# Local attention: the mask added by VectorE in the operation that takes the row extreme, instead of by mask products on TensorE

## What is computed

```python
q = l2norm(q) * qs
k = l2norm(k) * ksc
q, k = rotary_xpos(q, k)
...
bq = q.reshape(b, h, w, WINDOW, d) * QK_SCALE          # 8.0
bk, bv = (look_around(bk), look_around(bv))            # window before, window itself
sim = jnp.einsum('bhwid,bhwjd->bhwij', bq, bk)
mask = (i < j) | (i > j + WINDOW) | (j == -1)
sim = jnp.where(mask, -jnp.finfo(sim.dtype).max, sim)
attn = jax.nn.softmax(sim, axis=-1)
out = jnp.einsum('bhwij,bhwjd->bhwid', attn, bv)
```

## Time and profile before

| | |
|---|---|
| median of 3 runs | 2368.93 us (2366.84 to 2369.19) |
| profiled execution | 2361.52 us, its span 2359.7 us |
| busy: TensorE / VectorE / ScalarE / GpSimd | 1962.5 (83%) / 1318.0 (56%) / 1012.6 (43%) / 528.9 us (22%) |
| local attention, layer 0 and layer 1 | about 1103 to 1400 us and 1553 to 1850 us |
| L1369, two layers | 64 reductions, 1216 ns each |
| L1450, two layers | 256 exponentials, 483 ns each |
| L1568, score products, two layers | 512 TensorE instructions |

### The profile page before, as it was taken

The page is one execution under the profiler, slowest core; times in us unless marked ns, Lnnn a source line. Parts: engine busy times, 40 slices in busy tenths (PEclk is TensorE's granted clock), DMA queues, the critical chain, the costliest instruction groups (busy, mean ns, idle before and its releaser), DMA issues. The chain is left out here.

```text
span 2359.7 us, 32440 instructions
## 1 busy us (share of the span) xinstructions
PE 1962.5 (83%) x11804; PEld 1240.0 (53%) x11836; DVE 1318.0 (56%) x2301; ACT 1012.6 (43%) x2111; POOL 528.9 (22%) x893
## 2 busy tenths in 40 slices
PE   3788888888799797896899979979999899874595
PEld 1335555555467465574465655535566455442494
DVE  3548888888623498232666643236666333885412
ACT  1238888888621242211465641116565211432121
POOL 2102222222332300232222210112222110222321
PEclk9889999999999899998999999989999999986797
DMA  2243111110000100002000000030000000027395
GB/s 67 71 132 113 43 39 37 38 37 2 1 1 0 54 1 1 0 1 89 5 1 1 1 1 0 1 105 1 1 1 1 1 1 0 15 56 198 113 308 153
DMA packets 99133, 99.60 MB, mean 42 GB/s; under 512 B 33740, under 2 KB 83232, under 8 KB 98848
## 3 DMA queue, kind: packets, MB, share of 16 engines
q1 hardware_dynamic: 95904, 93.21, 13.2%
q0 software_dynamic: 3072, 4.34, 1.0%
HBM read 80.60 MB, written 16.92 MB: 41 GB/s over the span
## 5 line engine op out<-in xcount | busy, mean ns | idle before, releaser
L515 DVE TENSOR_REDUCE negmax<-sps 128x1 f32<-128x1024 f32 x256 | 307.6, 1212 | 21.6 <-PE sps L466 20.9
L559 ACT ACTIVATE prob<-sps,negmax 128x1024 f32<-128x1024 f32 x256 | 286.2, 1118 | 8.7 <-DVE negmax L515 6.1
L475 PE MATMUL sps<-ident,prob 128*128 128x128 f32 x1152 | 182.2, 287 | 57.0 <-ACT prob L559 56.1
L475 PEld LDWEIGHTS sps<-ident,prob 128*128 128x128 f32 x1152 | 134.7, 144 | 144.2 <-ACT prob L559 129.1
L604 POOL TENSOR_TENSOR probT<-probT,after 128x128 f32<-128x128 f32 x256 | 116.6, 455 | 281.5 <-DVE probT L523 191.3
L466 PE MATMUL sps<-ks,qs 128*128 128x512 f16 x512 | 162.1, 387 | 21.0 <-DVE ores L535 17.7
L568 ACT COPY probT<-sps 128x512 f32<-128x512 f32 (+1 forms) x192 | 101.6, 529 | 22.1 <-PE sps L475 22.1
L1304 POOL TENSOR_TENSOR la1qs<-la1qn,la1sin 128x256 f32<-128x256 f32 x64 | 60.3, 972 | 196.0 <-DVE la1qn L1381 196.0
L1304 POOL TENSOR_TENSOR la0qs<-la0qn,la0sin 128x256 f32<-128x256 f32 x64 | 60.3, 972 | 195.0 <-DVE la0qn L1381 195.0
L523 DVE COPY probT<-sps 128x512 f32<-128x512 f32 (+3 forms) x192 | 91.4, 476 | 4.7 <-PE sps L475 4.7
L491 PE MATMUL sps<-probT,vres 128*32 128x128 f32 x2304 | 82.5, 279 | 8.3 <-POOL probT L604 5.7
(11 more groups left out here) (450 smaller groups left out, 4246.2 us busy)
## 6 DMA issues: line engine op xcount, KB each, us to landing
w1e<-in_fc_T SPq DMA_DIRECT2D x16, 1024.0 KB, 6.6
w2e<-in_fc_T SPq DMA_DIRECT2D x16, 1024.0 KB, 9.6
qs<-q_parts SPq DMA_DIRECT2D x128, 64.0 KB, 1.9
ks<-k_parts SPq DMA_DIRECT2D x128, 64.0 KB, 1.9
q_parts<-parts SPq DMA_DIRECT2D x8, 512.0 KB, 3.6
k_parts<-parts SPq DMA_DIRECT2D x8, 512.0 KB, 5.4
token_rows<-r_row SPq DMA_DIRECT2D x4, 544.0 KB, 3.3
mixed<-r_zero SPq DMA_DIRECT2D x1, 2056.0 KB, 10.8
```

The lines of the kernel that those rows point to most:

```text
L475: mm = pe.transpose(slots[n % 4][:, at * P:(at + 1) * P], prob[:, n % 3, t * P:(t + 1) * P], ident[:])
L515: dve.tensor_reduce(negmax[:, n % 4:n % 4 + 1], slots[n % 4][:], X, ALU.max, negate=True).then_inc(s.max_done, 1)
L559: act.activation(prob[:, n % 3, :], slots[n % 4][:], ACT.Exp, bias=negmax[:, n % 4:n % 4 + 1], accum_out=rowsum[:, tile % 2, n % QUAD:n % ...
```

## The change

The scores' sign is turned: the table that holds the query scale has -8 in place of 8, so the scores come out negated, and masked places get +1e30 in place of -1e30. The mask products and the bf16 mask and identity tiles go. VectorE runs one fused operation per head: it adds the float32 mask to the head's 128 x 256 negated scores out of PSUM, writes the result to `prob` in SBUF, and gives the row's minimum to `nmax`. The minimum of the negated scores is the negated maximum, which the exponential takes as its bias as before; the exponential now reads and writes `prob` in place, with a scale of -1. `row_max` waits for the transposes that read `prob`, and `exponents` no longer does.

```diff
-        NEG = -1e30
+        FAR = 1e30
...
-                masks = sb(ph + "mb", [P, 2, 2, 2 * P], BF16, c)
-                identb = sb(ph + "ib", [P, P], BF16, c)
...
-                        pool.memset(maskf[:, 0, 0, :], NEG).then_inc(s.built2, 1)
+                        pool.memset(maskf[:, 0, 0, :], FAR).then_inc(s.built2, 1)
...
-                        pool.wait_ge(s.built2, 4)
-                        pool.tensor_copy(identb[:], ident[:]).then_inc(s.built3, 1)
-                        for first in range(2):
-                            for x in range(2):
-                                pool.tensor_copy(masks[:, first, x, :], maskf[:, first, :, :].rearrange("p a t -> p (a t)")).then_inc(s.built3, 1)
...
                                 dve.wait_ge(s.scores, 2 * t + half + 1)
-                                dve.tensor_reduce(nmax[:, half * HL // 2:(half + 1) * HL // 2],
-                                                  bs[:, half * 1024:(half + 1) * 1024].rearrange("p (s t) -> p s t", t=2 * P), X, ALU.max,
-                                                  negate=True).then_inc(s.max_done, 1)
+                                if t == 0 and half == 0:
+                                    dve.wait_ge(s.built2, 4)
+                                if t > 0:
+                                    dve.wait_ge(s.p_turned, 2 * t - 1 + half)
+                                for h in heads(half):
+                                    ins = dve.tensor_tensor_reduce(prob[:, h, :], bs[:, slot(h) * 256:(slot(h) + 1) * 256],
+                                                                   maskf[:, 1 if t % TPB else 0, :, :].rearrange("p a t -> p (a t)"),
+                                                                   1.0, FAR, ALU.add, ALU.min, nmax[:, h:h + 1])
+                                ins.then_inc(s.max_done, 1)
...
                             if t > 0:
                                 act.wait_ge(s.rinv_done, t)
-                                act.wait_ge(s.p_turned, 2 * t)
                             for half in range(2):
                                 act.wait_ge(s.max_done, 2 * t + half + 1)
                                 for h in heads(half):
-                                    ins = act.activation(prob[:, h, :], bs[:, slot(h) * 256:(slot(h) + 1) * 256], ACT.Exp,
-                                                         bias=nmax[:, slot(h):slot(h) + 1], accum_out=rsum[:, h:h + 1])
+                                    ins = act.activation(prob[:, h, :], prob[:, h, :], ACT.Exp, scale=-1.0,
+                                                         bias=nmax[:, h:h + 1], accum_out=rsum[:, h:h + 1])
...
-                            if t == 0:
-                                pe.wait_ge(s.built3, 5)
...
-                                for r in (2 * half, 2 * half + 1):
-                                    pe.matmul(bs[:, r * 512:(r + 1) * 512], identb[:],
-                                              masks[:, 1 if t % TPB else 0, :, :].rearrange("p x t -> p (x t)"),
-                                              start=True, stop=False, skip_group_check=True)
...
-                                                   start=False, stop=True, skip_group_check=True)
+                                                   start=True, stop=True, skip_group_check=True)
...
-    qk_scale = np.float32(8.0)
+    qk_scale = np.float32(-8.0)
```

More of the change, by code:

```diff
@@ L1232, in local_attention @@
                 bs = ps(ph + "bs", [P, 2048], c)
-                s = signals(ph, "@next_in @wo_in @w_in @tab_in @built1 @built2 @built3 @tab1 @x_turned @h_done @qk_done "
+                s = signals(ph, "@next_in @wo_in @w_in @tab_in @built1 @built2 @tab1 @x_turned @h_done @qk_done "
                             "@squared @ssum_done @norm_done @clipped @rnorm_done @normed @cos_done @sin_done "
@@ L1270, in _ @@
                         pool.wait_ge(s.built1, 5)
-                        pool.memset(maskf[:, 0, 0, :], NEG).then_inc(s.built2, 1)
-                        pool.affine_select(out=maskf[:, 1, 0, :], in_=maskf[:, 1, 0, :], compare_op=ALU.is_ge, fill=NEG,
+                        pool.memset(maskf[:, 0, 0, :], FAR).then_inc(s.built2, 1)
+                        pool.affine_select(out=maskf[:, 1, 0, :], in_=maskf[:, 1, 0, :], compare_op=ALU.is_ge, fill=FAR,
                                            base=0, pattern=[[1, P]], channel_multiplier=-1).then_inc(s.built2, 1)
                         for w in range(2):
-                            pool.affine_select(out=maskf[:, w, 1, :], in_=maskf[:, w, 1, :], compare_op=ALU.is_ge, fill=NEG,
+                            pool.affine_select(out=maskf[:, w, 1, :], in_=maskf[:, w, 1, :], compare_op=ALU.is_ge, fill=FAR,
                                                base=0, pattern=[[-1, P]], channel_multiplier=1).then_inc(s.built2, 1)
-                        pool.wait_ge(s.built2, 4)
-                        pool.tensor_copy(identb[:], ident[:]).then_inc(s.built3, 1)
-                        for first in range(2):
-                            for x in range(2):
-                                pool.tensor_copy(masks[:, first, x, :], maskf[:, first, :, :].rearrange("p a t -> p (a t)")).then_inc(s.built3, 1)
                         if l == 0:
```

## The result

| | before | after |
|---|---|---|
| median, runs on one chip | 2367.89 us (2365.28 to 2369.19) | 2398.64 us (2396.37 to 2400.94) |
| span of the profiled execution | 2359.7 us | 2396.8 us |
| mean granted clock of TensorE | 0.938 | 0.931 |
| busy: TensorE / VectorE / ScalarE / GpSimd | 1962.5 / 1318.0 / 1012.6 / 528.9 us | 1946.1 / 1333.5 / 1022.2 / 525.8 us |

The ratio is 1.0134, with an interval of 1.0117 to 1.0150: slower by 30.8 us. The prediction said 2390 (2373 to 2425).

The account below looks back on a forecast made before the run. A loop through ScalarE, VectorE and TensorE was taken as the bound, not TensorE alone. 28 tiles x (0.47 + 0.27) = 20.7 plus 0.8 in last tiles gave +21.5 us on 2368.9: 2390 us, range 2373 to 2425.

Parts of the forecast that it names:

- What bounds the kernel: Local attention: a loop of 8.6 us of ScalarE and VectorE in series and 8.45 us of TensorE, period 17.09.
- Part 1: TensorE's four mask products per tile go: 0 while the square sum precedes the extremes, -2.1 us over four last tiles.
- Part 2: VectorE: eight fused operations replace two reductions per tile, taken 0.40 us apart, adding 0.47 us to the loop.
- Half rate: Rival on VectorE: fused operations 0.67 us apart, +56 us, 2425 us; chance 0.11.
- Part 3: ScalarE's eight exponentials read SBUF in place, 0.034 us more each, +0.27 us in the loop.
- Part 4: Changed waits on ScalarE and VectorE: the table load still waits for the extremes, effect 0.
- What is late next: Behind the loop's later operations: reciprocal keeps some 0.3 us of waiting, widened inverse keeps 1 us of cover.
- The sum: Both layers: 20.7 us from 28 tiles and 0.8 from last tiles, together +21.5, giving 2390 us.
- The forecast's mechanism: Exponentials gated later with everything else hidden: 2390 us, own range 2375 to 2402; chance 0.68.
- The clock rival: TensorE's gaps grow and its clock dips, up to 1.7 us lost every 50 us: +19, 2409 us; chance 0.05.
- What would have shown it: Signs: period 17.8 us, operations 0.40 apart, load waiting 1.4, first transposes' wait about 1.5, TensorE busy down some 30.

Follow-up runs that it names:

- fused operations alone: Kernel after with the mask products kept and Exp reading the scores from PSUM as before: 2367.01 us, ratio 1.0031.
- waits exchanged, before: Kernel before with the wait for the extremes written ahead of those for the reciprocal and the transposes: 2335.26 us, ratio 0.9900.
- waits exchanged, after: Kernel after with the wait for the extremes written ahead of the one for the reciprocal: 2349.42 us, ratio 0.9967.
- products kept: Kernel after with the four mask products per tile put back ahead of the scores: 2379.26 us, ratio 1.0091.
- gap filled: Kernel after with three identity and mask products per tile, unused in the result, between the halves of the transposes: 2374.18 us, ratio 1.0060.
- no products: Kernel before with the four mask products per tile left out and nothing in their place: 2363.49 us, ratio 1.0023.

## Why the prediction was right, and where it was not

**What bounds the kernel: right.** One loop through ScalarE, VectorE and TensorE sets the period, and its TensorE part didn't change (8.49 and 8.48). A busy share of 95% was no bound.

**Part 1, the mask products: right.** They lay in TensorE's waiting: period 17.09 without them, and the last tiles' gain of 2 x 0.53 per layer came as 1.08. Their own time was taken a little short: 0.95 to 1.05 us in a tile, where the wait grew by 1.17 without them. What was missed is what came of that time: it turned into standing still, which the prediction counted as free in its sum.

**Part 2, the fused operations: right mechanism, mis-sized.** The operations start 0.345 apart and not 0.40, which makes the term 4 x 0.055 = 0.22 too large: the run with the fused operations alone shows +0.23 and not +0.47, near the lower bound of +0.20. The wrong step was the 0.06 for writing out the extreme, taken over from ScalarE. On VectorE it is a short operation of 0.08 of its own that runs while the next one starts. Half rate is ruled out: 0.42 us each, like L1393. The rule of the Trainium skill for two non-bf16 sources in SBUF ("Vector Engine (DVE) Microarchitecture Reference", section "Points that are easy to get wrong") wasn't in play, as the prediction read its wording: one source is PSUM here. No run here has the fused operation with both in SBUF.

**Part 3, Exp out of SBUF: right.** +0.04 each, 0.28 to 0.29 in the loop, where 0.27 was taken.

**Part 4, the waits: right.** The load still stood behind the extremes, waiting 1.18 (1.4 was expected, less by Part 2's error), and the exchange of two lines moved it. What is late next: the reciprocal kept its cover (0.55 of waiting, more than the 0.3 expected), and the widened inverse ended at 1219.46, before TensorE asked for it at 1220.65 without a wait.

**The sum: in part luck.** The longer operations are worth 14.0 us and not 21.5. The clock, which the sum took at nothing, is worth 15.3. The first error took 7.5 us off the second, so the time lies 9 us above the 2390 and within the forecast's own 2375 to 2402. The forecast's mechanism alone, rightly sized, would have given 2368.9 + 14.0 = 2383.

**The clock rival: it came, with 0.05 on it.** It was described rightly (waits of about 1.5 us, up to 1.7 us lost each time, one per 50 us, +19; measured: 1.62 us of waiting, 1.65 lost, seven in 24 steady tiles, mostly 54 us apart, +15). The failed step is its rejection. I looked only at the share of busy time (0.95 to 0.86) and at one 10 us window of the first attention that was still at 1.00, though its neighbour at 0.83 stood beside it. With what stood in those two rows, 1 in 20 was too little. It was also wrong to treat it as a rival of the forecast: the longer loop makes the waits longer (0.73 + 1.25 become 0.88 + 1.62), so the two come together.

**What would have shown it:** period of 17.8 (17.60), operations 0.40 apart (0.345), load waiting 1.4 (1.18), the wait ahead of the first transposes about 1.5 (1.62). Busy time of TensorE fell by 16.4 us and not 30: without the products alone it fell by 35.0 (1962.5 to 1927.5), and the stretches at half clock put about half of that back.

**What stays open:** by which measure the clock falls. The kernels order themselves by TensorE's standing still in a tile:

| kernel | waits in a steady tile, us | steady tiles of 19.0 us or more, of 24 |
|---|---|---|
| waits exchanged, before | 0 | 0 |
| before | 0.08 + 0.73 = 0.81 | 0 |
| fused operations alone | 0.30 + 0.73 = 1.03 | 0 |
| waits exchanged, after | 0.46 + 0.88 = 1.34 | 0 |
| products kept | 0.45 + 0.88 = 1.33 | 0 |
| gap filled | 1.62 + 0.23 = 1.85 | 1 (its waits: 1.90 + 0.22) |
| no products | 1.25 + 0.73 = 1.98 | 1 (its waits: 1.53 + 0.73) |
| after | 1.62 + 0.88 = 2.50 | 7 |

A 1.62 us wait alone doesn't bring it (gap filled, 23 tiles), while 1.53 + 0.73 did, so the longest wait by itself isn't the measure. Nor does the sum in the tile decide it: with products kept both tiles 0 wait 0.99 and 0.88 us, and layer 0's has a clock of 0.91 and layer 1's 1.00; and in the kernel after two of three tiles with 2.50 keep the full clock. The Trainium skill ("TensorE: Matmul & The Clock Gate", section "HAM oscillation — how this bites in real kernels") describes a kernel whose recurring waits throw the clock down in every pass. The same kind of thing is seen here, but in about every third tile (7 of 24) and not in each.

## What to carry to other kernels

Work can be taken off an engine that waits in every turn of a loop without any gain, and when that engine is TensorE it may cost: look at how long it will stand still per turn, and give the clock's fall a real chance when that grows. Price a fused operation from start to start, not by its length. And where an activation needs another function table, write first the wait that is due last, so that the load goes beside it: two exchanged lines gave 1.0% here, while the change under study lost 1.3%.

## What was new about the hardware

- TensorE's clock fell in 7 of 24 steady turns, mostly every third, of a loop of 17.6 us in which the engine stood still for 2.50 us, at the same places in two profiled executions, and cost 1.65 us each time, because the stretch at 1.2 GHz lay on the loop.
- VectorE's fused operation (128x256 float32 from PSUM and SBUF, with a row extreme) takes 0.42 us at 0.345 from start to start; the read of the extreme (0.08) is wholly covered by the next one.
- An Exp of 128x256 with a row sum starts 0.45 after the one before when it reads PSUM and writes SBUF, and 0.494 when it reads and writes SBUF in place.
- Of several waits ahead of an activation that needs a table load, the one written first goes with the activation, and the one written last holds up the load: late and last it held the load for 0.95 and 1.18 us, late and first it didn't. The exchange took 0.93 us off each tile of the kernel before and 1.13 us off each of the kernel after.
